# Sums of squares of the heads: accumulator outputs of ScalarE's squares in place of VectorE's row sums, under a new order of all engines

## What is computed

```python
mixed = silu(sum(xp[:, k:k + S, :] * conv_w[:, k] for k in range(4)))      # of x @ W_qkv
q, k, v = split(mixed)                                                     # q, k normalized per head
def step(St, inp):                                                         # over the chunks of the sequence
    v_new = u_i - kcd_i @ St
    out_i = (q_i * exp(g_i)) @ St + attn @ v_new
    St_new = St * exp(g_last) + (k_i * exp(g_last - g_i)).T @ v_new
    return St_new, out_i
var = mean(core * core, axis=-1, keepdims=True)                            # core: all out_i, per head
normed = core * rsqrt(var + EPS) * norm_w * silu(x @ W_z)
y = normed @ W_out
```

## Time and profile before

| | |
|---|---|
| time, median of 3 | 4364.57 us (4364.55 to 4368.52) |
| profiled execution | 4367.64 us, its span 4365.8 us |
| mean granted TensorE clock | 0.988 |
| TensorE busy | 4168.8 us, 95% of the span |
| VectorE busy | 3618.4 us, 83% |
| GpSimd busy | 3033.8 us, 69% |
| ScalarE busy | 2591.8 us, 59% |
| row sums L897 | 170.1 us in 256 instructions |
| squares L1251 | 160.2 us in 256 instructions |

### The profile page before, as it was taken

One profiled execution on the slowest core, in us unless ns is written; L12 is line 12 of the kernel. 1 busy time (PEld: TensorE's weight loads), 2 busy tenths in 40 slices (PEclk: granted clock), 3 DMA queues, 4 the chain that ended last, 5 costly groups with the idle time before them and its releaser, 6 DMA issues. The chain is left out here.

```text
span 4365.8 us, 91653 instructions
## 1 busy us (share of the span) xinstructions
PE 4168.8 (95%) x29748; PEld 3120.9 (71%) x29748; DVE 3618.4 (83%) x7996; ACT 2591.8 (59%) x5684; POOL 3033.8 (69%) x8984
## 2 busy tenths in 40 slices
PE   5699999999999999999999999999999999998798
PEld 2477777777777777777777777777777777776465
DVE  6588888888888988888888988888888888886554
ACT  3466666666666666666666666666666666665221
POOL 1577777777777777777777777777777777776221
PEclk8899999999999999999999999999999999999899
DMA  4333333333333333332333333333333323331100
GB/s 138 70 85 86 69 84 76 90 85 67 82 92 87 72 81 77 88 95 67 82 92 89 73 79 78 87 96 67 84 88 89 88 64 81 83 77 41 69 15 25
DMA packets 877310, 342.30 MB, mean 78 GB/s; under 512 B 741920, under 2 KB 826400, under 8 KB 867616
## 3 DMA queue, kind: packets, MB, share of 16 engines
q1 hardware_dynamic: 876832, 336.43, 31.5%
HBM read 255.44 MB, written 80.86 MB: 77 GB/s over the span
## 5 line engine op out<-in xcount | busy, mean ns | idle before, releaser
L735 DVE SCALAR_TENSOR_TENSOR CV<-pp,CW,CV 128x1023 f32<-128x1023 f32 (+2 forms) x768 | 978.5, 1274 | 25.3 <-ACT CV L1126 18.3
L380 PE MATMUL pp<-A,W 128*128 128x512 f32 x2048 | 974.6, 599 | 13.6 <-DVE CV L735 12.1
L1410 POOL TENSOR_TENSOR UL<-UL,TM 128x126 f32<-128x126 f32 (+22 forms) x1984 | 737.5, 372 | 155.5
L1407 POOL TENSOR_TENSOR TM<-UL,XL 128x126 f32<-128x126 f32 (+22 forms) x1984 | 704.3, 355 | 140.8 <-issue 11.2
L1226 ACT ACTIVATE VS<-qa,EB 128x128 f32<-128x128 f32 x1024 | 320.3, 365 | 465.4 <-PE qa L507 465.4
L878 DVE SCALAR_TENSOR_TENSOR St<-St,TAB,kv 128x128 f32<-128x128 f32 x1024 | 309.5, 344 | 345.3 <-PE kv L517 340.3
L380 PEld LDWEIGHTS pp<-A,W 128*128 128x128 f32 x2048 | 368.1, 193 | 283.1 <-issue 269.0
L561 PE MATMUL emit<-Wo,NTr 128*128 128x256 f32 x2048 | 498.6, 386 | 2.3 <-ACT NTr L1259 2.3
L540 PE MATMUL emit<-Wz,A 128*128 128x256 f32 x2048 | 494.9, 384 | 0.8 <-DVE A L929 0.8
L561 PEld LDWEIGHTS emit<-Wo,NTr 128*128 128x128 f32 x2048 | 374.6, 190 | 93.0 <-issue 29.7
L1215 ACT ACTIVATE QE<-qa,TAB 128x128 f32<-128x128 f32 x1024 | 317.6, 362 | 175.2 <-PE qa L497 173.5
(11 more groups left out here) (231 smaller groups left out, 8789.3 us busy)
## 6 DMA issues: line engine op xcount, KB each, us to landing
GB<-gcd SPq DMA_DIRECT2D x64, 1024.0 KB, 5.5
W<-wqkv SPq DMA_DIRECT2D x256, 128.0 KB, 3.5
XL<-xb SPq DMA_DIRECT2D x128, 256.0 KB, 3.9
kb<-TB SPq DMA_DIRECT2D x256, 128.0 KB
K<-kb SPq DMA_DIRECT2D x64, 512.0 KB, 5.1
UL<-c_u SPq DMA_DIRECT2D x64, 256.0 KB, 3.0
xb<-X SPq DMA_DIRECT2D x512, 32.0 KB, 1.6
Wz<-wz SPq DMA_DIRECT2D x64, 256.0 KB, 4.8
```

The lines of the kernel that those rows point to most:

```text
L380: ins = t.matmul(bk.pp[:, 512 * h:512 * h + 512], m.W[:, c, k, :], m.xnT[:, w // KH % 2, c, 512 * h:512 * h + 512], start=c == 0, stop=c == 1)
L735: v.scalar_tensor_tensor(m.CV[:, t, d:S], bk.pp[:, 0:S - d], m.CW[:, w % KH, t, 3 - d:4 - d], m.CV[:, t, d:S], ALU.mult, ALU.add).then_inc ...
L1407: gp.tensor_tensor(m.TM[:, 0:a, 0:b], m.UL[:, 0:a, k:k + 1].to_broadcast([128, a, b]), m.XL[:, k, k + 1:32].unsqueeze(1).to_broadcast([128 ...
L1410: gp.tensor_tensor(m.UL[:, 0:a, k + 1:32], m.UL[:, 0:a, k + 1:32], m.TM[:, 0:a, 0:b], ALU.subtract).then_inc(s["sub"], 1)
```

## The change

The squares of a quarter are four instructions over 128 columns each, and each gives its sum over the columns as accumulator output into a column of SC. JS still takes the squares. `red` and its semaphore are gone: tv waits for sq, and sq waits for the tv of two quarters before. Besides, the lists of calls of SyncE, TensorE, VectorE, ScalarE and GpSimd are in a new order within a pass.

```diff
-    def red(w, q):
...
-        dv.wait_ge(s["sq"], n + 1)
-        dv.wait_ge(s["tv"], n - 1)
-        v.tensor_reduce(m.SC[n % 2][:], m.JS[:], AXIS.X, ALU.add).then_inc(s["red"], 1)
...
         ac.wait_ge(s["core"], 2 * n + 2)
-        ac.wait_ge(s["red"], n)
-        a.activation(m.JS[:], m.CO[:, n % 2], ACT.Square).then_inc(s["sq"], 1)
+        ac.wait_ge(s["sq"], n)
+        ac.wait_ge(s["tv"], n - 1)
+        for u in range(4):
+            ins = a.activation(m.JS[:, u, :], m.CO[:, n % 2, u, :], ACT.Square, accum_out=m.SC[n % 2][:, u:u + 1])
+        ins.then_inc(s["sq"], 1)
...
-        po.wait_ge(s["red"], n + 1)
+        po.wait_ge(s["sq"], n + 1)
```

Of the lists, what the prediction speaks of (TensorE's late part first, then VectorE's, then SyncE's):

```diff
             at(u, 6)
-            op(u, 1)
             m1(u + 1)
+            z(u, 2)
             ks(u, 7)
...
             vn(u, 7)
-            z(u, 2)
+            pj(u + 2, 3, 0)
...
+            seed(u - 1, 3)
             s0(u)
-            red(u - 1, 3)
...
             nl(u + 1)
             ui(u + 2)
+            kto(u + 2)
+            ldo(u + 1)
+            kti(u + 2)
             xo(u + 2, 0)
```

More of the change, by code:

```diff
@@ L663, in loop @@
             ctp(u - 1, 3)
+            tpv(u + 1, 1, 0)
             ks(u, 2)
@@ L678, in loop @@
             at(u, 3)
-            tpv(u + 1, 1, 0)
+            ctp(u, 0)
             ks(u, 4)
             qs(u, 4)
-            ctp(u, 0)
             tpv(u + 1, 1, 1)
@@ L1040, in loop @@
             r_(u - 1, 2)
-            red(u - 1, 0)
             cvk(u + 1, 0, 2)
             oacc(u - 2, 3)
+            seed(u - 1, 0)
+            cvk(u + 1, 0, 3)
             state(u - 1, 2)
             core(u - 1, 2)
-            seed(u - 1, 0)
-            cvk(u + 1, 0, 3)
+            r_(u - 1, 3)
             ulr(u - 1, 1)
-            lm(u + 1, 0)
-            r_(u - 1, 3)
+            nrm(u - 1, 0)
             tq(u + 1)
-            nrm(u - 1, 0)
             state(u - 1, 3)
@@ L1057, in loop @@
             cvk(u + 1, 1, 2)
-            red(u - 1, 1)
             cvk(u + 1, 1, 3)
+            seed(u - 1, 1)
             state(u - 1, 4)
             core(u - 1, 4)
+            tk(u + 1)
             oacc(u - 1, 0)
-            tk(u + 1)
             r_(u - 1, 5)
-            seed(u - 1, 1)
+            lm(u + 1, 0)
             kra(u + 1)
+            krb(u + 1)
             state(u - 1, 5)
-            krb(u + 1)
             core(u - 1, 5)
-            r_(u - 1, 6)
+            nrm(u - 1, 1)
             x(u + 1, 0)
             att(u + 1, 0)
-            nrm(u - 1, 1)
-            red(u - 1, 2)
+            r_(u - 1, 6)
+            cvk(u + 1, 2, 1)
+            vt(u)
+            oacc(u - 1, 1)
+            state(u - 1, 6)
             x(u + 1, 1)
-            vt(u)
-            state(u - 1, 6)
+            att(u + 1, 1)
+            seed(u - 1, 2)
+            cvk(u + 1, 2, 2)
             core(u - 1, 6)
-            att(u + 1, 1)
             y1r(u)
-            cvk(u + 1, 2, 1)
             r_(u - 1, 7)
-            seed(u - 1, 2)
-            oacc(u - 1, 1)
-            cvk(u + 1, 2, 2)
             cvk(u + 1, 2, 3)
@@ L1096, in loop @@
             lm(u + 1, 2)
+            seed(u - 1, 3)
             s0(u)
-            red(u - 1, 3)
-            oacc(u - 1, 2)
-            seed(u - 1, 3)
-            lm(u + 1, 3)
             cvk(u + 1, 3, 1)
             r_(u, 0)
+            lm(u + 1, 3)
+            oacc(u - 1, 2)
             ulr(u, 0)
@@ L1346, in loop @@
             dec(u + 1, 0)
+            sq(u - 1, 2)
+            cv0(u + 1, 2)
+            qe(u - 1, 6)
+            nt(u - 1, 1)
             dec(u + 1, 1)
-            sq(u - 1, 2)
-            qe(u - 1, 6)
             vs(u - 1, 6)
             vne(u - 1, 6)
-            nt(u - 1, 1)
             dec(u + 1, 2)
-            cv0(u + 1, 2)
+            dec(u + 1, 3)
             y1l(u)
-            dec(u + 1, 3)
+            sz(u - 1, 2)
             qe(u - 1, 7)
@@ L1548, in loop @@
             sub(u + 1, 14)
+            sub(u + 1, 15)
+            on(u, 0)
+            sub(u + 1, 16)
+            sub(u + 1, 17)
             ixf(u + 2)
[L1550 to L1553 removed]
             sub(u + 1, 18)
```

73 lines of the change are left out of this document (31 added, 42 removed), and 2 rows, old and new, of the table SEMS.

## The result

The changed kernel takes 4529.91 us (median of 4 runs, 4524.16 to 4532.29), the kernel before, run again beside it, 4365.91: 1.0372 times as long, 95% interval 1.0357 to 1.0388. The forecast was 4371, in a range of 4332 to 4400: wrong by 159 us and outside the range. The profiled execution has a span of 4522.4 us.

What follows compares the result with a forecast made beforehand. TensorE was taken to bound the kernel (60.48 of a unit's 61.09 us). Terms 0.43 - 0.05 + 0.03 - 0.39 + 0.08 = +0.10 us a unit, times 62 is +6 on 4364.57: 4371 us, range 4332 to 4400.

Steps and rivals of the forecast that it cites:

- The squares: Four squares on ScalarE take 1.2 us in place of 0.63, 150 us more work; VectorE loses 170.1 us of row sums.
- The other estimate, 4 x 0.41 = 1.6: ScalarE's four squares by the Trainium skill's budget per ACTIVATE and element: 1.6 us, where the forecast took 1.2.
- squares too long: Rival: quarter 2's squares on ScalarE, at 1.6 us, delay cv0, NT and TensorE; 0.45 us a unit, 4393 us; chance 0.32.
- nothing but where something is queued behind a square: ScalarE's 150 us more was said to cost only there, as ScalarE is idle 21.7 of a unit's 61.09 us.
- (a): TensorE around chunk 4: one transpose group fewer between ks and vn, +0.43 us; a restart at chunk 2's ks goes, -0.05.
- (b): TensorE, sup of chunk 4 to ks of chunk 6: ks(5) stops waiting, nf waits 0.8 for P; +0.03 us a unit.
- (c): TensorE, kq(u+2,0) to m3: waits at op, m1, vn and z go, -0.39 us a unit; new handovers cost +0.08.
- GpSimd's own idle time, 14.5 us a unit, covers nk moved ahead of tv(u,2): GpSimd's new order, with the keys' norm steps ahead of quarter 2's tv, was counted at no cost.
- seed 0.15: Length in us of VectorE's seed of quarter 3, in a chain of lm, tv, seed and clearing done about 0.7 ahead of ks.
- The sign that the prediction itself named: The prediction called itself wrong if, among other signs, a wait for tv or seed reached TensorE.
- the row on VectorE that has no slack: VectorE row delayed with cv0 of tile 2 if the squares take 1.3 us or more; 0.35 us a unit at 1.6.
- less than 0.2 for nine handovers: VectorE's 1.7 us of slack over nine reordered handovers, less than 0.2 us each; counted +0.08, bounds 0 and 0.3.

Runs made afterwards that it cites:

- nothing held: Changed kernel with seeds and RK on GpSimd, quarter 2's Newton steps earlier, quarter 0's lm and GpSimd's second addition to GB later; 4356.0 us.

## Why the prediction was wrong, by its own steps

**The squares: right.** ScalarE works 142.5 us more (predicted 150); four squares take 1.17 us, and 1.27 with the last accumulator read (predicted 1.2). The other estimate, 4 x 0.41 = 1.6, did not come: a square of 128 columns takes 0.29 to 0.31 us. The rival "squares too long" needed 1.3 or more and did not come in the changed order, if only just. That the squares cost "nothing but where something is queued behind a square" is right too, but in the old order three things were: 63 to 67 us.

**(a): right at vn, its credit too small.** vn of chunk 4 starts 2.91 us behind at of chunk 3 (2185.68 and 2188.59 in the rows below; predicted 2.90), its wait grew by 0.44. But two restarts of 0.09 and smaller waits went with it, where 0.05 was counted: from m3 to sup of chunk 4 pass 31.55 us where 31.34 passed, 0.21 more and not 0.38. Whether these 0.21 could be had back is open, as the two runs that undid (a) each made something else late.

**(b): right.** No wait at ks(5), and nf's wait is 0.73 (predicted 0.8):

```profile
2185.68 0.61 PE L527 MATMUL qa<-VN,AT 128*128 128x128 f32 x4
...
2188.59 0.71 PE L507 MATMUL qa<-R,N 128*128 128x128 f32 x4 [0.47 <-DVE R L864]
...
2190.87 0.59 PE L517 MATMUL kv<-VS,K 128*128 128x256 f32 x2
...
2196.05 0.61 PE L507 MATMUL qa<-R,N 128*128 128x128 f32 x4
2197.22 0.41 PE L399 MATMUL strip<-cf,P 128*128 128x32 f32 x2 [0.56 <-DVE P L759]
...
2198.43 1.03 PE L410 MATMUL strip<-QK 128*128 128x256 f32 x4
```

nf is 6.35 us behind sup (6.44 predicted; before 6.86), and the next work 7.56 (7.66; before 7.63).

**(c): this is where it fell.** The stretch from kq(u+2,0) to m3 was to take 21.7 to 22.0 us. It took 22.30 in the mean before the change (22.17 in the unit read), and takes 24.76 in the changed kernel: the core, Y, pj, clock and AT of the table. In the kernel with nothing held it takes 21.96, 0.33 less than before (predicted -0.39 + 0.08). That kernel also has its seeds, Newton steps and second addition at other places, so it shows that the stretch can be had at the predicted length, not that the change as it stands would have had it.

**The step that failed** is the one that let GpSimd's part go at nothing: "GpSimd's own idle time, 14.5 us a unit, covers nk moved ahead of tv(u,2)". The change moves nk, tv and the second addition past each other on GpSimd, and the seed of quarter 2 on VectorE; I asked only what each waits for and whether the engine has the time (it has). All dependences were met in time, tv by 2 us. What was not asked is what runs on GpSimd at the moment when VectorE issues a short instruction between SBUF tiles. For the seed of quarter 2 that was nothing before, where GpSimd stood idle, and an addition of 2.35 us after; for RK an addition of 0.76 or a scaling of 1.89. The seed's price, "seed 0.15", was read from undisturbed rows, though the same line had cases of up to 419 ns in the trace of before, next to GpSimd's instructions of 0.4 us: the mechanism was there to be read, at a fifth of its later size. The sign that the prediction itself named, that a wait for the seed would reach TensorE, came true, by way of core.

The second failure is the range. Of my rivals one was a late row on VectorE at this very place ("the row on VectorE that has no slack", less than 0.2 for nine handovers), priced at 0.45 us. Once a row there is 2 us late, the price is the lateness less the slack, and the clock's fall adds to it: 2.5 us and not 0.45.

**The sum, put right** (units cut at nf, by which the unit of before is 61.26 us in the mean and the one after 63.87): 61.26; +0.21 for (a), -0.09 for (b), -0.33 for (c), and 61.04 with nothing held. From there to the changed kernel +2.80, all of it in (c): core 1.23, Y 0.16, pj 0.25, the clock 0.57, AT 0.44 and 0.15 in small ones; and 0.02 in (b), where lm stands elsewhere. Against the +0.10 of the forecast stand -0.22 with nothing held.

What stays open is how much of the 0.33 in front of pj belongs to RK's hold. It goes with AT's lateness, whatever makes that: 0.29 to 0.39 in the seven runs in which TensorE waits 0.36 us or more for AT, also where RK is short (the run with GpSimd's order of before), and 0.14 to 0.18 in the four in which it waits 0.10 or less.

## What to carry to other kernels

Before moving an instruction of GpSimd, or one of VectorE that is a tensor_scalar between SBUF tiles or has two inputs there, lay the two engines' timelines beside each other at the new place: a GpSimd instruction of 2.4 us can hold a VectorE one of 0.16 us until it ends, though neither depends on the other. The remedies, by what they gave here: put the long one where VectorE issues no such instruction (4530 to 4401 with one line), make the short one on GpSimd itself (4383), or cut the long one (4389); and look again after each, since the long one may meet the next short one (4407).

Accumulator outputs in place of a row sum are no gift: they move work to another engine's queue, and the order there has to be laid for it (4436 against 4372 with the same arithmetic).

## What the runs showed of the hardware

- A VectorE tensor_scalar between SBUF tiles, or one with two SBUF inputs, is held to the end of the long GpSimd instruction under way: 0.16 us became 2.11, 1.18 with the GpSimd instruction cut in two, 0.12 became 1.82 behind a scaling of 1.89, and all 812 such rows in 14 traces ended just behind GpSimd's. Transposes and row sums from SBUF, and instructions with an input in PSUM, kept their lengths. In the trace it is a long row, not idle time before a row, so no list of waits shows it.
- An accumulator output on ScalarE is an instruction of its own of 0.19 us that overlaps with the next square: four squares of 128 columns are spaced 0.29 us and take 1.27 us in all; without it, one of 512 columns takes 0.63.
- TensorE's waits of 1.57 us, with the shorter ones for Y and R behind them, were followed by a stretch at half the clock in 27 of 43 units; the run with GpSimd's order of before waits 1.00 us for AT in every unit, and its clock does not fall up to 4082.9.
